# Mixing stage of a two-layer spectral network: weights in pieces of 512 bytes with the surplus copied on chip, and the first chunk fetched one stage earlier

## The reference

```python
x = x + _L0_conv_ref(_gn(x), ...)
x = x + _L1_conv_ref(_gn(x), weight_real, weight_imag)

# _L1_conv_ref; weight_real and weight_imag are (32, 32, 128, 65)
weight = jax.lax.complex(weight_real, weight_imag)
multiplier = symmetric_padding(weight, im_shape, im_shape)
x_ft = symmetric_padding(rfftshift(jnp.fft.rfft2(x, norm='forward')), im_shape, im_shape)
out_ft = jnp.einsum('bixy,ioxy->boxy', x_ft, multiplier)
out = jnp.fft.irfft2(irfftshift(out_ft), s=im_shape, norm='forward')
```

## Time and profile before

| | us |
|---|---|
| median of 3 runs | 1078.45 |
| lowest and highest | 1077.09, 1087.74 |
| the profiled execution | 1081.58 |
| its span, first to last instruction | 1079.9 |
| busy: PE | 802.2 |
| busy: DVE | 682.8 |
| busy: ACT | 403.6 |
| busy: POOL | 368.1 |

### The profile page before, as it was taken

The page is one execution under the profiler, slowest core; times in us unless marked ns, Lnnn a source line. Parts: engine busy times, 40 slices in busy tenths (PEclk is TensorE's granted clock), DMA queues, the critical chain, the costliest instruction groups (busy, mean ns, idle before and its releaser), DMA issues. The chain is left out here.

```text
span 1079.9 us, 36766 instructions
## 1 busy us (share of the span) xinstructions
PE 802.2 (74%) x16050; PEld 588.2 (54%) x16050; DVE 682.8 (63%) x1459; ACT 403.6 (37%) x914; POOL 368.1 (34%) x262
## 2 busy tenths in 40 slices
PE   0499494699999954999923999467777777776797
PEld 0365241122222224888813999467666766666686
DVE  4897498478888885466658899635544544453132
ACT  0298342022222245555533566333333332332121
POOL 0022472589999910111100000324444444442000
PEclk9999697599999976999955999789888888888899
DMA  9566620494556430354231566579999999999587
GB/s 364 111 188 158 149 46 0 146 335 154 192 168 195 130 88 6 95 178 115 57 72 39 159 193 183 126 157 265 266 266 266 264 269 261 269 262 188 167 254 214
DMA packets 270191, 189.40 MB, mean 175 GB/s; under 512 B 29252, under 2 KB 259365, under 8 KB 268901
## 3 DMA queue, kind: packets, MB, share of 16 engines
q1 hardware_dynamic: 189571, 131.51, 45.9%
q10 hardware_dynamic: 75426, 44.17, 17.1%
q0 software_dynamic: 5120, 12.75, 4.2%
HBM read 154.48 MB, written 33.07 MB: 174 GB/s over the span
## 5 line engine op out<-in xcount | busy, mean ns | idle before, releaser
L2007 PE MATMUL po<-pa,room 128*32 128x16 f32 x8320 | 146.9, 221 | 85.4 <-DMA room<-_L_conv_weight_imag_dram 55.9
L2007 PEld LDWEIGHTS po<-pa,room 128*32 128x32 f32 x8320 | 144.4, 163 | 93.1 <-issue 61.1
L982 POOL TENSOR_TENSOR q<-wb,xb 128x1536 f32<-128x1536 f32 (+1 forms) x51 | 170.4, 3365 | 42.1 <-DMA wb<-wv 30.5
L1052 DVE TENSOR_TENSOR q<-pw,xb 128x1536 f32<-128x1536 f32 (+1 forms) x85 | 140.8, 1704 | 25.7 <-PE acc L1022 15.5
L1022 PE MATMUL acc<-q,pt 128*32 128x384 f32 (+1 forms) x1088 | 104.4, 496 | 15.3 <-DVE q L1052 15.3
L2148 DVE TENSOR_TENSOR osl<-po,neg 128x128 f32<-128x128 f32 x64 | 18.4, 288 | 150.3 <-ACT neg L2081 150.3
L1960 POOL DMA_DIRECT2D os_<-osl x64 | 45.4, 715 | 183.0 <-DVE osl L2159 175.0
L1950 POOL COPY cols<-y 128x512 f32<-128x512 f32 x32 | 38.3, 1196 | 147.7 <-POOLq L1716 142.0
L2081 ACT ACTIVATE neg<-po 128x272 f32<-128x272 f32 x32 | 12.7, 397 | 197.3 <-issue 182.6
L1994 PE MATMUL px<-wbat,cols 128*32 128x130 f32 x2176 | 75.8, 291 | 4.3 <-DVE wbat L2119 3.0
L1022 PEld LDWEIGHTS acc<-q,pt 128*32 128x32 f32 x1088 | 27.8, 110 | 91.1 <-issue 57.5
(11 more groups left out here) (334 smaller groups left out, 1586.2 us busy)
## 6 DMA issues: line engine op xcount, KB each, us to landing
room<-_L_conv_weight_real_dram ACTq DMA_DIRECT2D x32, 520.0 KB, 9.9
room<-_L_conv_weight_imag_dram ACTq DMA_DIRECT2D x32, 520.0 KB, 12.6
room<-_L_conv_weight_real_dram SPq DMA_DIRECT2D x32, 520.0 KB, 7.0
room<-_L_conv_weight_imag_dram SPq DMA_DIRECT2D x32, 520.0 KB, 10.6
xb<-xns SPq DMA_DIRECT2D x64, 192.0 KB, 3.2
wb<-wv SPq DMA_DIRECT2D x16, 576.0 KB, 5.9
yall<-in_x_dram SPq DMA_DIRECT2D x4, 2048.0 KB, 14.4
xd<-in_x_dram SPq DMA_DIRECT2D x16, 512.0 KB, 4.3
```

The lines of the kernel that those rows point to most:

```text
L982: nc.gpsimd.tensor_tensor(q2[:, t % 2, :, :, 0:m], bc(weights(blk, n), 2, NB), spectra(blk), ALU.mult).then_inc(s_qp, 1)
L1052: V.tensor_tensor(q1[:, t % 2, :, :, 0:m], bc(pw[t % 4][:, 0:3 * m].rearrange("p (r m) -> p r m", r=3), 2, NB), spectra(blk), ALU.mult).th ...
L2007: e = nc.tensor.matmul(po[u][32 * g:32 * g + 32, 512 * q + 16 * m:512 * q + 16 * m + 16], wsl[u][:, :, q * KWF + KWF - 1 - kw], xsl[u][:, ...
```

## The change

The change has five parts.

1. **Pieces of 512 bytes.** Chunks are joined in runs of eight (`RUN`; the last run of p = 0 has seven). The rows of a run lie one behind another in the weight tensors, 8 x 130 = 1040 floats for each channel pair, and are cut into one piece of 144 floats and seven of 128, in place of eight pieces of 130. There are as many transfers as before, with as many pieces and the same bytes in a run.
2. **Surplus copied.** A piece of a run brings floats of its neighbours: chunk j of a run holds 2(8 - j) floats that belong to the next. Before chunk c is mixed, DVE (p = 0) and ACT (p = 1) copy them from the buffer of chunk c - 1 into that of chunk c (`lap`, 64 x 32 x 14 elements down to 64 x 32 x 2). The copy stands at the head of `rows`, and waits until all four transfers of chunk c - 1 have landed. The pieces of one partition now lie 576 bytes apart. A buffer may be filled again only when the copy out of it is done, so SP and ACT wait for `s_xa` and `s_xd` (rows of the chunk before) as well before they issue.
3. **The first chunk in the row stage.** SP issues chunk 0 of p = 0 behind the loads of group 7, and that of p = 1 behind those of group 11. The two small matrices `gmean` and `wide` are loaded behind group 3. The two large tiles `room` and `pa` become one, `region`, so that the buffer of chunk 0 lies beside what the row stage reads.
4. **Moments.** ACT scales and sums in the row stage (four activations with a sum per group in place of two), and two reductions are left to DVE at the head of the mixing stage, in place of ten linked instructions. `wbat` is made in two instructions.
5. **The ends.** The matrices `eo` and `cf` of the last stage are loaded when the last chunk has been mixed. In the last chunk the two rows of p = 0 are not neighbours and come in transfers of their own, four in place of two with the same pieces of 260 bytes; half of them have their own semaphore (`s_wl`), for which DVE waits ahead of rows(31).

```diff
+RUN = 8
+LAP = 2 * RUN - 2
+PITCH = SM + LAP
+PIECE = 128
...
-        pa = keep("pa", [128, KW, 2, KH])
...
-        room = keep("room", [128, 4 * M2])
+        region = keep("region", [128, 6 * M2])
+        room = region[:, 0:4 * M2]
+        pa = region[:, 4 * M2:6 * M2].rearrange("p (w r h) -> p w r h", w=KW, r=2)
...
-        en8 = fwd.enter_context(nc.sbuf_tensor("en8", [128, 2, NGRP], F32))
-        spare = pa[:, :, :, :].rearrange("p w r h -> p (w r h)")[:, 0:2 * GI * WW]
+        WB, XS = NT * PITCH + LAP, 2 * NB * SL * 2 * KWF
+        base, sizes = 0, dict(w1=WB, w0=WB, xs0=XS, wbat=4 * NB * KWF, gmean=128, en8=4 * NGRP, mo=2 * NB, gs=3 * NB)
+        part = {}
+        for n, size in sizes.items():
+            part[n] = region[:, base:base + size]
+            base += size
+        assert base <= 6 * M2 and WB >= 2 * M2
+        wbuf = [part["w0"], part["w1"]]
+        wsl = [w[:, LAP:].rearrange("p (o m) -> p o m", o=NT) for w in wbuf]
+        wbat, gmean = part["wbat"].rearrange("p (b k) -> p b k", b=NB), part["gmean"]
+        en8 = part["en8"].rearrange("p (s g) -> p s g", s=4)
+        s_gm, s_wd, s_w = sem("group_matrix_loaded"), sem("forward_matrix_loaded"), sems("weight_chunk_loaded", 2)
+        s_wl = sem("last_row_weights_loaded")
+        spare = part["xs0"][:, 0:2 * GI * WW]
+
+        def run_of(p, c_):
+
+            first = c_ - c_ % RUN
+            return first, min(RUN, NCHK - 1 + p - first)
+
+        def load_weights(eng, p, c_):
+
+            u = c_ % 2
+            first, n = run_of(p, c_)
+            j = c_ - first
+            for r, w in enumerate((a["L1_conv_weight_real"], a["L1_conv_weight_imag"])):
+                q = slice(64 * p + 32 * r, 64 * p + 32 * r + 32)
+                if p == 0 and c_ == NCHK - 1:
+                    for row, dst, done in ((HH // 2, wsl[u][q, :, 0:KWF], s_w[u]), (HH - 1, wsl[u][q, :, KWF:SM], s_wl)):
+                        eng.dma_start(dst, bass.AP(w.tensor, row * KWF, [[NT * HH * KWF, NT], [HH * KWF, NT], [1, KWF]])).then_inc(done, 16)
+                else:
+                    size = PIECE if j else PIECE + 2 * n
+                    if p == 0:
+                        at = (HH // 2 + 1 + SL * first) * KWF + (PIECE * j + 2 * n if j else 0)
+                        to = 2 * (n - j) if j else 0
+                        dst = wsl[u][q, :, to:to + size]
+                    else:
+                        at = (HH // 2 - SL * first) * KWF - PIECE * (j + 1) - 2 * n
+                        to = LAP + 2 * (j + 1 - n)
+                        dst = wbuf[u][q, to:to + NT * PITCH].rearrange("p (o m) -> p o m", o=NT)[:, :, 0:size]
+                    src = bass.AP(w.tensor, at, [[NT * HH * KWF, NT], [HH * KWF, NT], [1, size]])
+                    eng.dma_start(dst, src).then_inc(s_w[u], 16)
+
+        def lap(p, c_):
+
+            first, n = run_of(p, c_)
+            k = 2 * (n - (c_ - first))
+            if c_ == first or p == 0 and c_ == NCHK - 1:
+                return None
+            q = slice(64 * p, 64 * p + 64)
+            new, old = wbuf[c_ % 2], wbuf[1 - c_ % 2]
+
+            def cut(buf, at):
+                if at < 0:
+                    return buf[q, LAP + at:LAP + at + NT * PITCH].rearrange("p (o m) -> p o m", o=NT)[:, :, 0:k]
+                return buf[q, LAP:].rearrange("p (o m) -> p o m", o=NT)[:, :, at:at + k]
+            return (cut(new, 0), cut(old, SM)) if p == 0 else (cut(new, SM - k), cut(old, -k))
...
-                each_batch(body)
+                body(0)
+                sp.dma_start(gmean, c["gmean"]).then_inc(s_gm, 16)
+                sp.dma_start(wbat[:, NB - 1], c["wide"]).then_inc(s_wd, 16)
+                for p in range(2):
+                    body(p + 1)
+                    load_weights(sp, p, 0)
+                body(3)
...
-                    act.activation(sq7[:, 0], y1[:, bass.ds(g * GI, GI), 0:64], ACT.Square, accum_out=en8[:, 0, bass.ds(g, 1)])
-                    act.activation(sq7[:, 1, :, 0:63], y1[:, bass.ds(g * GI, GI), 66:129], ACT.Square, accum_out=en8[:, 1, bass.ds(g, 1)]).then_inc(s_sq7, 1)
+                    G = slice(g * GI, g * GI + GI)
+                    act.activation(row0[:, :], y1[:, G, 0], ACT.Copy, scale=1.0 / NT, accum_out=en8[:, 0, g:g + 1])
+                    act.activation(sq7[:, 0, :, 0:63], y1[:, G, 1:64], ACT.Square, scale=math.sqrt(2.0 / NT), accum_out=en8[:, 1, g:g + 1])
+                    act.activation(sq7[:, 1, :, 0:63], y1[:, G, 66:129], ACT.Square, scale=math.sqrt(2.0 / NT), accum_out=en8[:, 2, g:g + 1])
+                    act.activation(sq7[:, :, :, 63].rearrange("w z i -> w i z"), y1[:, G, 0:65:64], ACT.Square, scale=math.sqrt(1.0 / NT), accum_out=en8[:, 3, g:g + 1]).then_inc(s_sq7, 1)
...
-                for t, n in ((gmean, "gmean"), (wide, "wide")):
-                    sp.dma_start(t[:, :], c[n]).then_inc(s_ld, 16)
-                for c_ in range(NCHK):
+                for c_ in range(1, NCHK):
                     wait(sp, s_ms, c_ - 1)
+                    wait(sp, s_xd, c_)
+                    wait(sp, s_xa, c_)
                     load_weights(sp, 0, c_)
+                sp.wait_ge(s_ms, NCHK)
                 for t, n in ((eo, "eo"), (cf, "cf")):
-                    sp.dma_start(t[:, :], c[n]).then_inc(s_eo, 16)
+                    sp.dma_start(t, c[n]).then_inc(s_eo, 16)
...
-                load_weights(act, 1, 0)
                 load_weights(act, 1, 1)
                 root.serve(act, nc.scalar, gs[:, 2, :])
                 act.wait_ge(s_zero, 2)
 
                 def rows(c_):
+                    wait(act, s_ms, c_ - 1)
+                    if lap(1, c_) is not None:
+                        act.wait_ge(s_w[1 - c_ % 2], 64 * ((c_ - 1) // 2 + 1))
+                        act.activation(*lap(1, c_), ACT.Copy)
                     act.wait_ge(s_sp, c_ + 1)
-                    wait(act, s_ms, c_ - 1)
                     for half in range(2):
                         src, re, im = spectrum_rows(c_, 0, half)
                         for b in range(2):
@@ -2076,6 +2121,8 @@
                 for c_ in range(NCHK):
                     act.wait_ge(s_ms, c_ + 1)
                     if c_ + 2 < NCHK:
+                        act.wait_ge(s_xa, c_ + 2)
+                        act.wait_ge(s_xd, c_ + 2)
                         load_weights(act, 1, c_ + 2)
...
-                ch.link(V.reduce_sum(mo[:, 0, :], y1[:, :, 0].rearrange("w (b i) -> w b i", b=NB), axis=AX.X))
-
-                ch.link(V.tensor_tensor(sq[:, :, :], y1[:, :, 0:65:64], y1[:, :, 0:65:64], ALU.mult))
-                ch.link(V.reduce_sum(en2[:, :, :], sq[:, :, :].rearrange("w (b i) k -> w b k i", b=NB), axis=AX.X))
-                ch.link(V.reduce_sum(mo[:, 1, :], en8[:, 0, :].rearrange("w (b q) -> w b q", b=NB), axis=AX.X))
-                ch.link(V.reduce_sum(enb[:, :], en8[:, 1, :].rearrange("w (b q) -> w b q", b=NB), axis=AX.X))
-                ch.link(V.tensor_tensor(mo[:, 1, :], mo[:, 1, :], enb[:, :], ALU.add))
-                ch.link(V.tensor_scalar(mo[:, 1, :], mo[:, 1, :], 2.0, None, ALU.mult))
-                ch.link(V.tensor_tensor(mo[:, 1, :], mo[:, 1, :], en2[:, :, 0], ALU.subtract))
-                ch.link(V.tensor_tensor(mo[:, 1, :], mo[:, 1, :], en2[:, :, 1], ALU.add))
-                V.tensor_scalar(mo[:, :, :], mo[:, :, :], 1.0 / NT, None, ALU.mult).then_inc(s_mo8, 1)
+                V.reduce_sum(mo[:, 0, :], en8[:, 0, :].rearrange("w (b q) -> w b q", b=NB), axis=AX.X)
+                V.reduce_sum(mo[:, 1, :], en8[:, 1:4, :].rearrange("w s (b q) -> w b s q", b=NB), axis=AX.XY).then_inc(s_mo8, 1)
                 for v in range(2):
                     V.memset(po[v][:, :].rearrange("p (q x) -> p q x", q=SL)[:, :, 256:272], 0.0).then_inc(s_oc, 1)
                 dve.wait_ge(s_gm8, 1)
@@ -2115,15 +2153,21 @@
                 ch.link(V.tensor_tensor(gs[:, 2, :], gs[:, 0, :], gs[:, 0, :], ALU.mult))
                 ch.link(V.tensor_tensor(gs[:, 2, :], gs[:, 1, :], gs[:, 2, :], ALU.subtract))
                 root.rsqrt(dve, ch, V, gs[:, 2, :], gs[:, 2, :])
-                dve.wait_ge(s_ld, 32)
-                V.tensor_tensor(wbat[:, :, :], bc(wide[:, :], 1, NB), bc(gs[:, 2, :], 2, 4 * KWF), ALU.mult).then_inc(s_wb, 1)
+                dve.wait_ge(s_wd, 16)
+                ch.link(V.tensor_tensor(wbat[:, 0:NB - 1], bc(wbat[:, NB - 1], 1, NB - 1), bc(gs[:, 2, 0:NB - 1], 2, 4 * KWF), ALU.mult))
+                V.tensor_tensor(wbat[:, NB - 1], wbat[:, NB - 1], gs[:, 2, NB - 1:NB].broadcast_to([128, 4 * KWF]), ALU.mult).then_inc(s_wb, 1)
                 y0 = y1[:, :, 0].rearrange("w (b i) -> w b i", b=NB)
                 V.tensor_tensor(y0, y0, bc(gs[:, 0, :], 2, NT), ALU.subtract).then_inc(s_b0, 1)
                 dve.wait_ge(s_zero, 2)
 
                 def rows(c_):
+                    wait(dve, s_ms, c_ - 1)
+                    if lap(0, c_) is not None:
+                        dve.wait_ge(s_w[1 - c_ % 2], 64 * ((c_ - 1) // 2 + 1))
```

(27 more changed lines are left out.)

21 lines of the change are left out of this document (2 added, 19 removed).

## The result

The changed kernel takes **1091.24 us** (median of 14 runs, 1088.33 to 1096.48). The kernel before, run beside it, takes 1081.41. The ratio is **1.0103, 95% interval 1.0088 to 1.0118**: slower by about 1%, where 1082 was predicted (range 1058 to 1098). The profiled execution has a span of 1088.1 us against 1079.9. All ratios here compare fast executions; the only slow one, of 1867.95 us, is one of six in experiment 4, and its ratio leaves it out.

A forecast was written before the change was run, and what follows sets the result against it. The mixing stage was taken as bound by the rate of incoming weight packets. Terms -1 + 0.5 - 5.5 + 6.0 + 0.6 + 3.2 = +3.8 us on the median of 1078.45 gave 1082.3 us; range 1058 to 1098, forecast's own 1077 to 1089.

The forecast's parts named there:

- pieces of 512 bytes: Mixing stage's weight transfers: a packet costs 28 ns at either size while both queues bring weights; -1 us at most.
- The faster rival (burst rate throughout): Weight transfers: 512-byte pieces come at 676 packets a microsecond all the time; -20 us, 1062 us, chance 0.29.
- the slower one (gap in SBUF): Weight transfers: each piece, now a write of its own, costs 11.5 ns more; +35 us, 1117 us, chance 0.15.
- the head: Begin of the mixing stage: cheaper moments let mix(0) start at 700.5 in place of 706.1; -5.5 us.
- Chunk 0 is there: Head of the mixing stage: the first chunk's weights have already landed when mix(0) needs them; no size of its own.
- the row stage: Chunk 0's weights between image loads delay the loads behind them, two stalls of 3.3 us; +6.0 us (1.5 to 7.6).
- +0.6 for ACT: Row stage: two more activations with a sum per group, hidden except in the last group; +0.6 us (0.4 to 0.9).
- TensorE hides some 0.3 us of each: Row stage: of each 3.3 us stall, TensorE hides some 0.3 us, within the sum of +6.0 us.
- the copies of surplus: Mixing stage: DVE's copies of 0.5 to 1.4 us and `rows` end just as the mix does; 0 to +0.1 us a chunk.
- The term of +0.5 for the stage: Mixing stage: copies of surplus and the two added waits on SP and ACT before each issue; +0.5 us (0 to 3).
- The prediction's model, issue, 12.7 us, mix, issue: Mixing stage's chain: issue, some 12.7 us of transfer, 4.5 us of mixing, next issue; links two chunks apart, 18.16 us.
- the end: Last chunk: rows(31) waits for all its weights, so its 3.2 us come after the transfer, no longer hidden; +3.2 us.

The follow-up runs named there:

- experiment 4: Changed kernel with pieces of 520 bytes in the same buffers, a gap of 56 bytes between them, and no copies of surplus: 1093.84 us, ratio 1.0096.
- experiment 5: Kernel before with only the moments moved to ACT in the row stage, two reductions left on DVE: 1080.85 us, ratio 0.9989.
- experiment 9: Experiment 6 with pieces of 520 bytes and no copies of surplus, in two versions: 1079.52 us (0.9967) and 1077.44 us (0.9960).
- experiment 1: Changed kernel with chunk 0 fetched at the mixing stage's begin, not in the row stage: 1084.68 us, ratio 1.0027.
- experiment 2: Changed kernel with chunk 0's four transfers in the row stage behind the last group's load: 1081.89 us, ratio 0.9998.
- experiment 3: Changed kernel with chunk 0's four transfers one by one behind the loads of groups 5, 7, 9 and 11: 1081.01 us, ratio 1.0010.
- Experiment 6: experiment 2 with DVE's wait for the last row's weights moved to ahead of the last copy only: 1077.19 us (0.9957), repeated 1077.62 us (0.9950).
- experiment 7: DVE's surplus copy made as a sum over a length-one axis: in the changed kernel 1096.27 us (1.0144), on top of Experiment 6 1081.17 us (0.9970).
- experiment 8: Changed kernel with each queue bringing both halves of the partitions, SP the real parts and ACT the imaginary ones: 1115.10 us, ratio 1.0304.

## Why the prediction was right and wrong

The time lies within the stated range of 1058 to 1098, but above the forecast's own, 1077 to 1089 (whose bounds in fact add up to 1088). What made room for it was half the price of a gap in SBUF, and that price was nil: being inside is luck. Of the 9 us between 1082 and 1091.24, 3 are the kernel before, whose median over 14 runs is 1081.41 and not the 1078.45 of the first three. The rest is this:

**Right: pieces of 512 bytes.** The step that decides, 28 ns a packet at either size, held (27.9 ns before and in the changed kernel): 9.09 us a chunk became 9.07. That makes 29 x 0.024 = 0.7 us where -1 was forecast, but the agreement says nothing: other executions with pieces of 512 bytes have 9.06 to 9.11, and the kernel of experiment 5, with 520, has 9.07. The faster rival (burst rate throughout) and the slower one (gap in SBUF) are both out, by the chunk distances of the traces and experiments 4 and 9.

**Right in size, wrong in its reason: the head.** -5.5 was forecast for mix(0), and it came 5.2 us sooner. The working put it all on the moments. Experiment 5 shows that they alone bring 2.0 us at mix(0), as the weights take 13.7 us to land, and experiment 1 that with the fetch at the stage's begin ACT's issues take the place of the moments. "Chunk 0 is there" stood in the prediction as an aside, and without it only 2.0 us of the term are left. Of the 5.2 us, 3.8 are left at mix(2).

**Wrong in size: the row stage.** This is the step that failed. +6.0 (1.5 to 7.6) and +0.6 for ACT were forecast, +11.0 was seen, and 12.7 at an equal start, more than the upper bound. The mechanism was right (experiments 1 to 3), and these terms of it were too small:
- The insert was priced at 348 packets a microsecond, from a row of 520-byte pieces. Chunk 0's are 576 bytes long and came at 322: 6.4 us and not 5.9. The prediction's own 11.5 ns a packet and 0.066 ns a byte give 323.
- A slack of 0.5 us was assumed, though the page showed DVE waiting 0.34 us for a load already: the slack was nil. 6.4 - 2.1 is 4.3 us, and 4.34 was the second wait. The first was 5.17: 4.3, the 0.34 of before, and some 0.5 us without an explanation.
- "TensorE hides some 0.3 us of each" had the wrong sign. Each stall reached TensorE and came back to DVE, 1.02 and 2.36 us. That makes 9.5 + 3.4 = 12.9 us of waits, for the 12.7 us by which the stage is longer at an equal start.
- ACT's +0.6 was 0.0 (experiment 5).
- That TensorE's clock at the stage's begin differs between executions, worth 1.6 us of the stage, was in no term.

**Missed, and without a price: the copies of surplus.** "At most 1.4 us" was taken from DVE's own rows. GpSimd was not looked at. Eleven of DVE's copies take up to 3.2 us, so `rows` ended 6 us after the landing and not "just as the mix does". The term of +0.5 for the stage was still not too low: the whole steady part moved by -0.7 us. The prediction's model, issue, 12.7 us, mix, issue, would have charged 1.3 us for each of them. It fails there because the packets' rate sets the distance of chunks, and the time from issue to landing gives way.

**Right: the end.** +3.2 forecast, +3.1 seen. Experiment 6 takes it back.

The sum on the steps seen is 11.0 - 5.2 + 0.7 (mix(0) to the last landing, which takes up what the head loses again by mix(2)) + 3.1 = +9.6 us, for the +9.8 between the medians (the two traces differ by 8.2, with the 2.5 less ahead of the row stage and the 1.2 more at the end; the ratio of 1.0103 is 11.1). The forecast was +3.8, and 4.4 of the missing 5.8 us are the row stage's.

What stays open: whether and why a late issue is more than made up (experiment 7), and what fills the holes of TensorE's first round. A third weight buffer, which would tell whether the low level of the rate can be avoided, was not tried.

## What to carry to other kernels

A prefetch costs what is queued behind it, not its bytes: the same four transfers cost 12.7 us of stage in front of loads without slack, 3.1 us one at a time, and 0 to 0.6 behind the last load. Price it by the packets of the half of the partitions that it writes, and put it last on its queue. Two parts that each remove one of two waits ending together (moments and first weights) are worth little alone, so look for the second wait before crediting the first. And a stage that is bound by a transfer rate gives a late issue back, so time won between landing and issue is not time won. Before you compare a stage between two traces, look whether it began at the same granted clock: here that alone was 1.6 us, more than some terms of the sum.

## What the runs showed of the hardware that was not expected

- A DVE copy of up to 448 elements a partition within SBUF takes 0.17 to 0.55 us with no GpSimd copy beside it, and 1.3 to 3.4 us beside one or two GpSimd copies of 1.2 us, until they have ended; as a reduction over an axis of length one it takes 0.21 to 0.63 us, also beside them.
- One queue on one half of the partitions has 348 packets a microsecond with pieces of 520 bytes (177 GB/s) and 322 with 576 (181 GB/s). Two queues on different halves have 574, and 366 (184 GB/s) in a stretch of experiment 8 where, judged by the rate, both write the same half.
- Of four transfers of 1024 packets that ACT issues in a row, the third and fourth hold it for 2.7 and 3.8 us in experiment 1 and for 1.3 and 3.2 in experiment 5 (0.6 us when little is queued), and with it all that stands behind on that engine.
- A packet of 512 bytes and one of 520 cost the same (27.9 ns for each engine's packet, with both queues busy), also with gaps of 56 bytes between the destinations (9.13 us a chunk for 9.09).
- The same 32 products at the row stage's begin take TensorE 3.50 us at a granted clock of 0.54 and 1.97 at 1.00, and which of the two a kernel meets changes from execution to execution.
